# Two expert slabs instead of one copied by ScalarE and weighed on GpSimd, and the order of four engines laid out anew

## The reference

```
xn   = layernorm(x)                       # over the 64 channels
q,k,v,g = xn@Wq, xn@Wk, xn@Wv, xn@Wg      # 4 heads of 32
sim  = q·k/sqrt(32) + bias(xn@Wb), masked; attn = softmax(sim)
x    = x + ((attn·v) * sigmoid(g)) @ Wo
t    = layernorm(x)
p    = softmax(t@router_w + router_b); the two largest of 8, rescaled to sum 1
x    = x + sum over the two experts of p_e * (t@expert_w[e] + expert_b[e])
```

## Time and profile before

| what | value |
|---|---|
| median of three runs | 954.86 us |
| profiled execution, its span | 954.15 us, 952.3 us |
| busy share of PE, DVE, POOL, ACT | 83%, 81%, 70%, 51% |
| one step in the middle | 19.1 us |
| starts of row_max half 0 of groups 2, 3, 4, 5 | 166.71, 183.90, 202.25, 221.30 us |
| TensorE's granted clock, mean | 0.975 |
| PE, from a piece's start to the next: spread_inverse pair, a gate half, project_v, turn2, router | 0.56, 0.28, 0.44, 0.28, 0.32 us |
| the same: project_out, a turn_max, turn_coef, expert_bias | 0.62, 0.10, 0.10, 0.15 us |
| DVE, the same: weigh, qk_low, share 6 and 7, route 10 to 12, finish, rest_max | 0.60, 0.40, 0.60, 0.51, 0.40, 0.09 us |
| DVE, the same: attention_out, total2; POOL: norm2's three instructions | 0.40, 0.40; 2.2 us |

### The profile page before, as it was taken

The page is one execution under the profiler, slowest core; times in us unless marked ns, Lnnn a source line. Parts: engine busy times, 40 slices in busy tenths (PEclk is TensorE's granted clock), DMA queues, the critical chain, the costliest instruction groups (busy, mean ns, idle before and its releaser), DMA issues.

```text
span 952.3 us, 40372 instructions
## 1 busy us (share of the span) xinstructions
PE 791.2 (83%) x15174; PEld 500.7 (53%) x15174; DVE 767.4 (81%) x1808; ACT 487.8 (51%) x1061; POOL 663.4 (70%) x1092
## 2 busy tenths in 40 slices
PE   1444147999999999999999999999999999999753
PEld 1333123666665666666656665666566656565521
DVE  7776553588889888988898889888888888888764
ACT  3777113465555554655465546554655465546411
POOL 7899000257777767777777777767776777677877
PEclk9999998999999999999999999999999999999965
DMA  3554310000110011001100110011001100100000
GB/s 115 181 194 166 101 39 23 24 23 31 51 38 30 28 48 34 28 28 48 34 28 28 47 36 28 28 48 34 28 28 41 41 28 28 46 32 24 17 13 17
DMA packets 38088, 44.76 MB, mean 47 GB/s; under 512 B 6416, under 2 KB 32656, under 8 KB 38032
## 3 DMA queue, kind: packets, MB, share of 16 engines
q1 hardware_dynamic: 38032, 43.99, 13.9%
HBM read 14.48 MB, written 9.83 MB: 26 GB/s over the span
## 4 chain that ended last, share of the span: by engine, by line
PE 34%; DVE 34%; issue 20%; POOL 8%; ACT 1%; DVEq 1%; DMA 1%; SPq 0%; POOLq 0%; ACTq 0%
DVE negm L800 6%; PE psS L1068 6%; DVE rinv L816 4%; PE psS L1043 4%; POOL ln_s L393 4%; DVE prod L915 3%; PE ps_o L1125 3%; PE ps_x L1125 2%; PE ps_x L1128 2%; PE ps_o L1128 2%; DVE og L831 2%; DVE rt L877 2%; DVE q_lo L792 2%; POOL xn L396 2%; DVE ogu L823 1%
## 5 line engine op out<-in xcount | busy, mean ns | idle before, releaser
L443 POOL TENSOR_TENSOR add<-prod 128x256 f32<-128x256 f32 x160 | 116.3, 727 | 100.7 <-DVE prod L915 100.7
L800 DVE TENSOR_REDUCE negm<-psS 128x12 f16<-128x1920 f32 x80 | 146.0, 1825 | 12.0 <-PE psS L1053 8.2
L494 ACT ACTIVATE hl<-xn 128x320 f16<-128x320 f32 (+1 forms) x60 | 33.5, 559 | 158.3 <-POOL xn L396 156.8
L393 POOL TENSOR_TENSOR ln_s<-ln_v,half 128x5 f32<-128x5 f32 (+1 forms) x60 | 97.0, 1616 | 4.7
L448 POOL TENSOR_TENSOR add<-add 128x128 f32<-128x128 f32 x200 | 91.0, 455 | 0.1
L425 POOL TENSOR_TENSOR rinv_lo<-rinv,rinv_hi 128x160 f16<-128x160 f32 x40 | 19.7, 492 | 100.9 <-ACT rinv_hi L564 100.9
L533 ACT ACTIVATE pt_b<-psS 128x1920 f32<-128x1920 f32 x40 | 70.8, 1771 | 19.6 <-PE psS L1087 15.6
L450 POOL TENSOR_TENSOR ymix<-add 128x64 f32<-128x64 f32 x200 | 64.3, 322 | 15.7
L489 ACT ACTIVATE sq<-xc 128x320 f32<-128x320 f32 (+1 forms) x60 | 33.3, 556 | 81.7 <-POOL xc L409 73.1
L431 POOL TENSOR_TENSOR og_lo<-og,og_hi 128x320 f16<-128x320 f32 x80 | 61.6, 791 | 17.3 <-ACT og_hi L570 17.3
L1043 PE MATMUL psS<-bm,ident 128*128 128x480 f16 (+1 forms) x320 | 68.4, 337 | 5.9 <-ACT pt_a L533 3.3
(11 more groups left out here) (263 smaller groups left out, 2819.3 us busy)
## 6 DMA issues: line engine op xcount, KB each, us to landing
xin<-in_x SPq DMA_DIRECT2D x20, 320.0 KB, 2.9
xs_all<-xs_pair SPq DMA_DIRECT2D x20, 320.0 KB, 2.5
xs_q<-xs_all SPq DMA_DIRECT2D x40, 160.0 KB, 2.1
xs_v<-xs_all SPq DMA_DIRECT2D x40, 160.0 KB, 2.1
xin<-in_x SPq DMA_DIRECT2D x40, 160.0 KB, 2.2
out<-res SPq DMA_DIRECT2D x40, 160.0 KB, 1.9
bias_scratch<-b_stage SPq DMA_DIRECT2D x20, 160.0 KB, 2.4
pt_a<-bias_scratch SPq DMA_DIRECT2D x1, 320.0 KB, 3.2
```

The costliest lines, as they stand in the source:

```text
L393: pool.tensor_tensor(ln_s[a][:, 3, 0:w], ln_v[a][:, 0:w], half[:, 0:w], ALU.pow).then_inc(own, 1)
L443: pool.tensor_tensor(add1[t % 2][:], prod_of(t)[:, 0:4, :], prod_of(t)[:, 4:8, :], ALU.add).then_inc(mix_step[t], 1)
L800: dve.tensor_reduce(negm[c][:, :, 0:slots], psS[:, :, 0:slots * N].rearrange("i h (s j) -> i h s j", s=slots), AX.X, ALU.max, negate=True) ...
```

## The change

Slabs 1 and 3 take the way over `kept`, instead of slab 2. Slab 2 is weighed by DVE. The tile `kept` is still one, so within a group `keep_expert(3)` now waits until `mix_halves(1)` has read it, where the wait before was on the previous group alone. Routing steps 4 to 12, the shares and `finish` move to the next step (lag 5 for finish), `project_out` and `attention_out` to other places, and the steps are in a new order on PE, DVE, ACT and POOL; banks are handed out anew. SyncE's order is the same. The loop covers steps 9 to 36, and there is one step more at the end.

```diff
-KEPT = (2,)
+KEPT = (1, 3,)
-        FIRST, LOOP, LOOP_END, LAST = -2, 7, GROUPS - 3, GROUPS + 4
+        FIRST, LOOP, LOOP_END, LAST = -2, 9, GROUPS - 3, GROUPS + 5
...
-                need(act, mix_step[KEPT[KEPT.index(t) - 1]], 3 * (g - 1) + 1)
+                i = KEPT.index(t)
+                if i > 0: act.wait_ge(mix_step[KEPT[i - 1]], 3 * g + 1)
+                else: need(act, mix_step[KEPT[-1]], 3 * (g - 1) + 1)
...
-                if on(n - 4): finish(n - 4, a, ps_m)
+                if on(n - 5): finish(n - 5, b, ps_x)
...
-                if on(n - 2): project_out(n - 2, ps_m)
+                if on(n - 1): project_out(n - 1, ps_m)
```

More of the change, by code:

```diff
@@ L928, in step @@
                 b = 1 - a
-                if on(n - 1): gated(n - 1, b, 0, ps_o)
-                if on(n - 4): finish(n - 4, a, ps_m)
[L931 to L935, removed]
+                for k in range(4, 7):
+                    if on(n - 3): route(n - 3, k)
+                for k in range(7, 10):
+                    if on(n - 3): route(n - 3, k)
@@ new lines, in step @@
+                if on(n - 2): normed(n - 2, 0, ps_r)
+                if on(n - 2): normed(n - 2, 1, ps_x)
+                for k in range(10, 13):
+                    if on(n - 3): route(n - 3, k)
+                if on(n - 5): finish(n - 5, b, ps_x)
+                if on(n + 1): qk_low(n + 1, b, 0, 0, ps_r)
+                if on(n): row_max(n, 1)
+                if on(n - 1): invert(n - 1, ps_x)
+                if on(n - 2): attention_out(n - 2, a, ps_m)
+                if on(n - 2): total2(n - 2, a)
@@ L936, in step @@
+                if on(n - 2): mean2(n - 2, a)
+                for k in range(1, 3):
+                    if on(n - 3): share(n - 3, k)
+                for k in range(3, 6):
+                    if on(n - 3): share(n - 3, k)
+                if on(n + 1): qk_low(n + 1, b, 1, 0, ps_o)
+                if on(n - 2): sumsq2(n - 2, a)
+                if on(n + 1): qk_low(n + 1, b, 0, 1, ps_x)
+                if on(n + 1): qk_low(n + 1, b, 1, 1, ps_r)
                 for k in range(6, 8):
                     if on(n - 3): share(n - 3, k)
-                if on(n - 3): weigh(n - 3, 4, ps_o)
@@ L939, in step @@
[L939 to L942, removed]
+                if on(n - 1): gated(n - 1, b, 1, ps_x)
+                if on(n - 3): weigh(n - 3, 0, ps_r)
+                if on(n - 1): gated(n - 1, b, 0, ps_m)
+                if on(n + 1): row_max(n + 1, 0)
+                if on(n - 3): weigh(n - 3, 2, ps_r)
+                if on(n - 2): logits(n - 2, ps_o)
@@ L943, in step @@
+                if on(n + 1): rest_max(n + 1)
                 for k in range(1, 4):
                     if on(n - 2): route(n - 2, k)
[L945 to L951, removed]
-                if on(n + 2): qk_low(n + 2, a, 1, 1, ps_o)
@@ L953, in step @@
-                for k in range(1, 3):
-                    if on(n - 2): share(n - 2, k)
-                if on(n - 1): attention_out(n - 1, b, ps_m)
-                for k in range(3, 6):
-                    if on(n - 2): share(n - 2, k)
-                if on(n - 1): total2(n - 1, b)
-                if on(n - 2): weigh(n - 2, 0, ps_m)
-                if on(n - 1): mean2(n - 1, b)
-                if on(n + 2): qk_low(n + 2, a, 0, 1, ps_x)
-                if on(n + 2): row_max(n + 2, 0)
-                if on(n - 1): sumsq2(n - 1, b)
@@ L964, in step @@
-                if on(n - 2): weigh(n - 2, 1, ps_r)
+                if on(n - 3): weigh(n - 3, 4, ps_x)
             run_steps(dve, step)
@@ L1246, in step @@
+                if on(n + 2): project_qk(n + 2, a, 0, 0, ps_r)
+                if on(n - 4): expert_bias(n - 4, ps_x)
                 if on(n + 1): max_scores(n + 1, b, 1)
-                if on(n + 1): project_gate(n + 1, b, 1, ps_m)
+                if on(n): row_sums(n, a, ps_x)
+                if on(n + 1): turn_max(n + 1, 0, ps_o)
                 if on(n - 3): turn_coef(n - 3, ps_r, banks16[2])
-                if on(n - 2): experts(n - 2, a, 2, ps_o)
-                if on(n - 2): router(n - 2, a, ps_x)
@@ L1256, in _ @@
+                if on(n - 2): experts(n - 2, a, 1, ps_m)
             pe.wait_ge(w_ready, 1)
```

88 lines of the change are left out of this document (44 added, 44 removed).

## The result

The changed kernel takes 976.34 us (median of four runs, 975.51 to 979.49), the kernel before 953.69 (four runs, 951.77 to 955.25): a ratio of 1.0236, 95% interval 1.0209 to 1.0263. It is 2.4% slower. The forecast was 943 us.

The account below looks back on a forecast made before the run. A ring through TensorE and VectorE, its longest piece 9.13 us of VectorE, was taken as the bound. 36 x (19.10 - 18.9) = 7.2, less 0.6, plus 4.6: 11.2 off 954.15 gives 942.95, forecast 943 us, range 932 to 957.

Parts of the forecast that it names:

- The phase is one like before in kind, so I stay near today's amount and take 0.15 more: VectorE's routing stretch: GpSimd hold-ups stay near today's 0.8 us, plus 0.15, giving 18.9 us a step.
- The ring: New order's chain of waits through TensorE, ScalarE and VectorE: 9.00 + 1.00 + 8.70 = 18.70 us a step.
- the 201 ns cases: Routing products on VectorE that ran in 201 ns, taken as disagreeing with the rule of mutual exclusion with GpSimd.
- The upper bound of 20.8 us: Step time if eight two-input VectorE instructions each wait half of a 0.72 us GpSimd instruction, 2.9 us in all.
- The whole stretch from row_max 0's end to rinv's end: VectorE's work there takes 9.04 us, against 9.00 for TensorE's ring, making VectorE's ring 18.74 us.
- rival 3: Much faster: TensorE's gaps half covered and VectorE held up less, 18.3 us a step, 921 us; chance 0.08.
- the allowance of 0.13: Added on TensorE, without a row, because the attends now stand apart, each followed by f16 work: 0.13 us a step.
- 4.6 us won in the draining: End of the last group: 64.8 instead of 69.4 us, center 6.7 earlier, two more kept weighings costing 2.1.
- the filling: Early steps of the loop take 17.9 and 18.3 us, so 0.6 us is lost.
- rival 2: Slower: four of eight two-input VectorE instructions wait half a 0.72 us addition, 19.4 us a step, 961 us; chance 0.14.
- Two signs of the forecast: TensorE waits about 0.4 us for exponent ahead of max_scores 1, about 0.3 for rinv ahead of the projection behind turn_max 1.
- The high2 path: ScalarE's high2 needs GpSimd's norm2, with keep_v_rest and turn2 behind: slack 0.5 us, any excess added to the step.

Follow-up runs that it names:

- e1: Changed kernel with GpSimd's fifteen mixing additions a group cut to one column, each followed by a time-filling memset, sums of the experts left out: 921.95 us, ratio 0.9655.
- e9: Changed kernel, full work, GpSimd additions merged and laid beside VectorE's PSUM work by waits, rest_max moved ahead of finish: 947.32 us, ratio 0.992.
- e10: Changed kernel with GpSimd's additions merged, in the changed kernel's order, no added waits, rest_max where it was: 958.99 us, ratio 1.0041.
- e7: Changed kernel with both GpSimd weighings of kept slabs cut to one column of 64, order unchanged: 954.58 us, ratio 0.9995.
- e11: As e10, but rest_max moved from behind row_max 0 to ahead of finish: 966.52 us, ratio 1.0119.
- e5: Changed kernel, same work: GpSimd's mix_halves of slabs 2 and 3 wait for routing points, og_low moved earlier, rest_max ahead of finish: 1007.94 us, ratio 1.0565.
- e6: As e5, but rest_max stays behind row_max 0: 1005.49 us, ratio 1.0535.
- e3: Changed kernel with keep_v_rest ahead of high2 on ScalarE, so turn2 no longer waits for it: 975.33 us, ratio 1.0217.
- e2: Kernel before the change with the same one-column additions and memsets as e1, sums of the experts left out: 948.76 us, ratio 0.9943.
- e4: Kernel before the change with share 6 and 7 moved ahead of normed, into VectorE's pause ahead of og: 954.03 us, ratio 0.9992.

## Why the prediction was wrong

**The step that failed** is "The phase is one like before in kind, so I stay near today's amount and take 0.15 more". It isn't alike. The ring was walked to within 0.4 us, the hold in it was sized by its old neighbours. What one instruction of each routing line takes (ns, minimum/median/maximum), before:

```profile
L870 DVE TENSOR_TENSOR rt<-lg,rs x40: 199/201/354, 194.8 to 933.6; 128x40 f32<-128x40 f32 x40
L871 DVE TENSOR_TENSOR rt<-rt,order x40: 200/204/714, 195.1 to 933.9; 128x40 f32<-128x40 f32 x40
...
L873 DVE TENSOR_TENSOR rt<-rt,rs x40: 199/200/203, 196.1 to 934.9; 128x40 f32<-128x40 f32 x40
L874 DVE SCALAR_TENSOR_TENSOR rt<-rt,lg x40: 201/310/675, 196.3 to 935.1; 128x40 f32<-128x40 f32 x40
...
L877 DVE TENSOR_TENSOR rt<-rt,rs x40: 199/486/490, 196.8 to 935.7; 128x40 f32<-128x40 f32 x40
```

and after:

```profile
L874 DVE TENSOR_TENSOR rt<-lg,rs x40: 199/567/570, 190.2 to 957.0; 128x40 f32<-128x40 f32 x40
L875 DVE TENSOR_TENSOR rt<-rt,order x40: 201/649/652, 190.5 to 957.6; 128x40 f32<-128x40 f32 x40
...
L877 DVE TENSOR_TENSOR rt<-rt,rs x40: 200/762/770, 190.9 to 958.9; 128x40 f32<-128x40 f32 x40
L878 DVE SCALAR_TENSOR_TENSOR rt<-rt,lg x40: 199/381/384, 191.2 to 959.7; 128x40 f32<-128x40 f32 x40
...
L882 DVE TENSOR_TENSOR rt<-rt,order x40: 199/336/380, 191.9 to 960.6; 128x40 f32<-128x40 f32 x40
```

Before, the five shown and L878 last 2.12 us together by their medians, 0.92 more than six at 0.20. After, the five and L881, which stays at 0.20, last 2.90, 1.70 more; with am's 0.37 it is 2.07, so 1.15 more than before. I had booked 0.15. In the old order the routing's first products ran beside GpSimd's short second and third additions (0.46 and 0.32 us), and only the last two of them beside og_low (0.78); in the new order rest_max runs beside a weighing of 1.04, the first three products beside additions of 0.72, and two more beside additions of 0.46.

**The rule was there and I set it aside.** I wrote that the 201 ns cases speak against the Trainium skill's rule ("SBUF — State Buffer", "Who interferes with whom"). They don't: there VectorE had started first, or GpSimd's instruction ended within the 0.2 us anyway. This case's traces agree with the rule nearly throughout: two SBUF inputs are held (am, the products), a reduce and an instruction with one PSUM input are not, and a GpSimd memset holds nobody (e1). Only the power of 1.18 us (L393), which reads SBUF too, holds nobody either, and there the measurement decides. The upper bound of 20.8 us was priced wrongly as well: half of a 0.72 us instruction for each of eight made 2.9 us, where six held ones cost 2.07 and the rest nothing. That these six come to 0.35 us each, near my 0.36, is luck. They follow each other, and one that starts just behind the start of a GpSimd instruction is held for nearly its whole length (L877: 0.76 us beside an addition of 0.73), while one that starts late loses little (L882: 0.14 us).

**The sum, term by term.** The whole stretch from row_max 0's end to rinv's end was forecast at 9.04 us plus 0.15. It became 10.13 (503.37 to 513.50) and 10.45 in turn, 10.27 in the mean: 1.08 more. The rest of the ring was some 0.25 us shorter than walked. So the step became 19.72 instead of 18.9; over 36 steps 30 us of the 33 by which the forecast missed. That this stretch sets the step shows in all runs of the changed order (means over the steps of the loop, us):

| run | row_max 0's end to rinv's end | a step | difference |
|---|---|---|---|
| e1 | 8.84 | 18.31 | 9.47 |
| e9 | 9.34 | 18.88 | 9.54 |
| e10 | 9.67 | 19.20 | 9.53 |
| e7 | 9.71 | 19.18 | 9.47 |
| e11 | 10.02 | 19.42 | 9.40 |
| changed kernel | 10.27 | 19.72 | 9.45 |
| e5 | 8.86 | 20.49 | 11.63 |

Only e5 (and e6 with it) falls out, by the wait for residual and the clock. Without the holding of the additions (e1) the ring is 18.31, which is rival 3's number: the walk of 18.70 was 0.4 too long. 0.2 of it lie in the stretch (8.84 instead of 9.04), and 0.2 between rinv and the end of the next row_max 0, where the attends with what stands around them take 2.87 us (516.42 to 519.29) and not 3.11, the allowance of 0.13 included.

**The ends.** I had 4.6 us won in the draining. e1 shows it: 76.7 us behind the last row_max 0 (844.24 to 920.9) against 81.5 before, so 4.8; in the changed kernel the holding in the draining steps gives them back (81.3). The last group's center came 37.3 us after its scores 0 (909.13 to 946.42), where I had said about 35. Of the filling I had 0.6 us lost, it is 3.6. About 2.5 of them are there already at the first row_max 0 (136.82 against 134.26); in e3, with one place of ScalarE's order changed, it stands at 134.83. Why it comes later I haven't tried to find out.

**The rivals.** What happened is rival 2 in place and mechanism, with 19.72 instead of its 19.4 us a step: 976 instead of 961 us. Its threshold (0.47 us of extra holding) was passed more than twice over, with 1.15; its chance of 0.14 and the range up to 957 were too low. The sign the prediction named for it came: og 5.3 to 5.5 us after row_max 0's end, where over 4.5 was to mean a held routing. Two signs of the forecast didn't: TensorE was to wait some 0.4 us for exponent ahead of max_scores 1 and some 0.3 for rinv, and it waits 1.3 for og instead, two pieces earlier. VectorE's 1.50 us pause at og is gone, as forecast; the one ahead of gated is 0.68 us, not 1. The high2 path was tight as said (TensorE waits 0.21 us ahead of turn2 in every second step) and cost nothing that could be measured (e3). keep_expert(3) wasn't late in a way that shows: exponent's wait is for its scores.

## What to carry to other kernels

Where VectorE and GpSimd work side by side, list for each small VectorE instruction with two SBUF inputs which GpSimd instruction is under way when it starts; its price in these traces is what that one has left, not a share of its own length, so an order of work must be read on both engines together. Moving such a chain onto the critical ring beside GpSimd's longest instructions cost 1.4 us in 18.3 here, and the order that is the faster one without the additions' holding (18.31 us a step, against 18.97 in e2) is the slower one with it. What helped was to merge GpSimd's additions and to lay its long ones beside VectorE's work on PSUM (e9); pauses put into GpSimd alone (e5) made its last result late for somebody else, and the pause that this gave TensorE cost clock as well.

## What the runs showed of the hardware

- The hold doesn't depend on the size of the held instruction: am, with 16 values, took 0.57 us, 0.78 at most in the rows above, against 0.17 where GpSimd stood elsewhere (e7).
- A copy with conversion from SBUF to SBUF is held as well, although it has one input (0.60 us in e4, against 0.19 in the changed kernel, where it stands beside the power). The reduces of the same size never were.
- A GpSimd instruction that only writes holds no two-input instruction: in e1 GpSimd was busy for 33.84 of 40 us, with memsets beside the routing, and none of the two-input instructions that started beside a memset took over 0.20 us.
- Nor does every GpSimd instruction that reads SBUF hold: beside the power of 5 values, 1.18 us long, 36 of 36 two-input instructions in the changed kernel kept their length.
- A pause of TensorE of some 1.5 us can cost clock: in 9 of 35 steps of e5 some 3 us at 0.50 (the 1.2 GHz level) follow it, in the others none.
